# Key and value placement by DMA in the fourth layer of an attention kernel on one Trainium2 core

## What is computed

```python
residual = x
qt = conv1x1(x, w_q, b_q).reshape(BS * N_HEADS, H * W, -1)
xp = avg_pool_3x3_s2_same(x)                      # 8x8 tokens per image
kt = conv1x1(xp, w_k, b_k).reshape(BS * N_HEADS, H * W // 4, -1)
vt = conv1x1(xp, w_v, b_v).reshape(BS * N_HEADS, H * W // 4, -1)
attn = jnp.einsum('bnd,bmd->bnm', qt, kt) / TEMP  # d = 16
attn = jax.nn.softmax(attn, axis=-1)
out = jnp.einsum('bnm,bmd->bnd', attn, vt).reshape(BS, H, W, -1)
return conv1x1(out, w_o, b_o) + residual
```

## Time and profile before

| | |
|---|---|
| median of 3 runs | 147.38 us (146.55 to 152.97) |
| the profiled execution's own time | 146.52 us |
| its span in the trace | 144.6 us |
| PE busy | 132.7 us, 92% of the span |
| DVE busy | 105.5 us, 73% |
| ACT busy | 103.4 us, 72% |
| POOL busy | 57.4 us, 40% |

### The profile page before, as it was taken

One profiled execution on the slowest core, in us unless ns is written; L12 is line 12 of the kernel. 1 busy time (PEld: TensorE's weight loads), 2 busy tenths in 40 slices (PEclk: granted clock), 3 DMA queues, 4 the chain that ended last, 5 costly groups with the idle time before them and its releaser, 6 DMA issues.

```text
span 144.6 us, 4108 instructions
## 1 busy us (share of the span) xinstructions
PE 132.7 (92%) x1615; PEld 104.5 (72%) x1615; DVE 105.5 (73%) x249; ACT 103.4 (72%) x286; POOL 57.4 (40%) x91
## 2 busy tenths in 40 slices
PE   7677999999999999779698999999998999999991
PEld 4447999977676767555576996858665766899890
DVE  5775888998226979997588657799999997920062
ACT  0435734799883779869985599999899987676530
POOL 8941994000000000000078888105058776499000
PEclk9999999999999999999999999999999999999999
DMA  4950000000000000000000000000000000000036
GB/s 128 328 204 0 0 7 0 0 2 0 0 5 0 5 0 5 0 0 0 0 5 0 7 0 5 0 0 5 0 0 5 0 5 0 5 5 5 5 99 192
DMA packets 5026, 3.69 MB, mean 26 GB/s; under 512 B 400, under 2 KB 4880, under 8 KB 5008
## 3 DMA queue, kind: packets, MB, share of 16 engines
q1 hardware_dynamic: 3376, 1.78, 4.3%
q10 hardware_dynamic: 1632, 1.66, 3.6%
HBM read 2.39 MB, written 1.05 MB: 24 GB/s over the span
## 4 chain that ended last, share of the span: by engine, by line
PE 63%; DVE 26%; DMA 3%; issue 3%; POOL 1%; ACT 1%; ACTq 0%; DVEq 0%
PE bank L678 10%; PE bank L737 8%; PE bank L623 6%; PE bank L717 5%; PE bank L725 5%; DVE negmax L471 4%; PE bank L689 4%; DMA x_all<-in_x_dram 3%; DVE prob L480 3%; PE bank L662 3%; DVE prob L513 3%; PE bank L696 3%; PE bank L754 3%; DVE probT L494 3%; PE bank L609 2%
## 5 line engine op out<-in xcount | busy, mean ns | idle before, releaser
L332 ACT ACTIVATE prob<-bank,negmax 128x256 f32<-128x256 f32 (+1 forms) x48 | 19.4, 414 | 13.1 <-DVE negmax L471 12.8
L273 POOL TENSOR_TENSOR prob<-prob,inv 128x512 f32<-128x512 f32 x16 | 16.3, 1043 | 19.2 <-DVE inv L523 19.2
L285 POOL TENSOR_TENSOR prob<-xT 128x128 f32<-128x128 f32 x8 | 3.4, 419 | 49.5 <-DVE xT L504 49.4
L678 PE MATMUL bank<-probT,v 128*128 128x256 f32 x64 | 17.0, 388 | 1.8 <-issue 1.8
L623 PE MATMUL bank<-packed,xT 128*128 128x128 f32 x96 | 15.6, 287 | 1.0 <-ACT prob L332 1.0
L340 ACT ACTIVATE kdiag<-prob 32x512 f32<-32x512 f32 x24 | 15.0, 627 | 1.5 <-DVE prob L562 1.2
L717 PE MATMUL bank<-kdiag,qT 128*32 128x256 f32 x256 | 15.5, 382 | 0.0
L623 PEld LDWEIGHTS bank<-packed,xT 128*128 128x128 f32 x96 | 13.2, 191 | 2.9 <-issue 2.0
L678 PEld LDWEIGHTS bank<-probT,v 128*128 128x128 f32 x64 | 10.9, 190 | 4.6 <-issue 3.8
L501 DVE SCALAR_TENSOR_TENSOR xT<-bank,packed,xT 128x256 f32<-128x256 f32 x16 | 7.5, 482 | 7.8 <-PE bank L678 6.7
L471 DVE TENSOR_REDUCE negmax<-bank 128x2 f32<-128x512 f32 (+1 forms) x24 | 12.8, 534 | 0.5 <-PE bank L652 0.3
(11 more groups left out here) (92 smaller groups left out, 294.6 us busy)
## 6 DMA issues: line engine op xcount, KB each, us to landing
out_dram<-x_all SPq DMA_DIRECT2D x8, 128.0 KB, 1.9
packed<-in_pack_dram ACTq DMA_DIRECT2D x1, 708.5 KB, 6.9
x_all<-in_x_dram SPq DMA_DIRECT2D x2, 256.0 KB, 4.6
x_all<-in_x_dram ACTq DMA_DIRECT2D x2, 256.0 KB, 5.6
packed<-in_pack_dram SPq DMA_DIRECT2D x1, 198.0 KB, 5.9
packed<-in_pack_dram ACTq DMA_DIRECT2D x1, 192.0 KB, 6.2
packed<-in_pack_dram ACTq DMA_DIRECT2D x1, 160.0 KB, 3.2
packed<-in_pack_dram ACTq DMA_DIRECT2D x1, 48.0 KB, 5.8
```

The costliest lines, as they stand in the source:

```text
L273: nc.gpsimd.tensor_tensor(p, p, inv[g][:, t, :].unsqueeze(2).broadcast_to([128, HEADS, KEYS]), ALU.mult)\
L332: last = nc.scalar.activation(prob[g][:, t, 0:keys], psum("scores", layer, g)[:, keys * t:keys * t + keys], ACT.Exp, bias=negmax[g][:, t, ...
L678: last = mm(ps[:, 0:TOK], vals[:, k, :], probT[g][:, 0, TOK * k:TOK * k + TOK], start=k == 0, stop=k == TILES - 1)
```

## The change

The fourth layer's keys and values of a pair of images are each projected once, with unrepeated weights: one product of 128 columns for keys (channels on partitions) and one for values (tokens on partitions), in one bank. ACT adds the key bias into `kT`, DVE the value bias into `vt`. SP writes both to DRAM tensors `k_rows` and `v_rows`. It waits for each and places the keys with eight DMAs (one for each chunk's 16 partitions) into `kdiag`, now a block diagonal of all eight chunks, and the values with two DMAs into `vdiag`. Queries are unpadded: one product of 256 columns and one ACT instruction. A score product has 512 columns and there are 4 for a token tile instead of 8; its moving operand reads `kdiag` with a step of 128 elements (512 bytes) from one element to the next. There are two `kdiag` buffers instead of four, so pairs 2 and 3 wait for the scores of pairs 0 and 1 before they are placed. The step `vd` is gone. In the table `q` comes before `kv`, and `scores3` keeps its distance from `pool`.

```diff
-        steps += [("pool", 3, 1), ("kv", 3, 3), ("q", 3, 3), ("vd", 3, 1), ("scores3", 3, 1), ("share3", 3, 2), ("probT3", 3, 2),
+        steps += [("pool", 3, 1), ("q", 3, 3), ("kv", 3, 0), ("scores3", 3, 5), ("share3", 3, 2), ("probT3", 3, 2),
...
+            for step, layer, g in sequence:
+                if step == "kv":
+                    i = g // PAIR
+
+                    sp.wait_ge(s_key_rows, i + 1)
+                    sp.dma_start(k_dram[i], kT[i][:, :]).then_inc(s_keys_out[i], 16)
+                    wait_drained(sp, "kv", 3, g)
+                    sp.dma_start(v_dram[i], vt[i][:, :]).then_inc(s_vals_out[i], 16)
+                    if i == 0:
+                        sp.wait_ge(s_zero, QUARTERS + IMAGES // PAIR)
+                    if i >= KEY_BUFFERS:
+                        for t in range(TILES):
+                            wait_filled(sp, f"scores{t}", 3, PAIR * (i - KEY_BUFFERS) + PAIR - 1)
+                    sp.wait_ge(s_keys_out[i], 16)
+                    rows = k_dram[i].rearrange("(c e) n -> e c n", e=DH)
+                    for c in range(HEADS):
+                        sp.dma_start(kdiag[i % KEY_BUFFERS][DH * c:DH * c + DH, c, :, :], rows).then_inc(s_keys[i], 16)
+                    sp.wait_ge(s_vals_out[i], 16)
+                    rows = v_dram[i].rearrange("(j m) (c e) -> (m c) j e", m=HEADS, e=DH)
+                    for c2 in range(2):
+                        sp.dma_start(vdiag[i][KEYS * c2:KEYS * c2 + KEYS, :, c2, :], rows).then_inc(s_vals[i], 16)
...
-            def kv_strips(g):
-                for k in range(2):
-                    wait_drained(act, f"kv{k}", 3, g)
-                    for b in range(DVE_STRIPS, STRIPS):
-                        last = nc.scalar.activation(*kv_strip(g, k, b), ACT.Copy)
-                last.then_inc(s_strips_act, 1)
+            def keys3(g):
+                wait_filled(act, "kv", 3, g)
+                nc.scalar.activation(kT[g // PAIR][:, :], psum("kv", 3, g)[:, 0:PAIR * PTOK], ACT.Identity, bias=part["bk3"])\
+                    .then_inc(s_key_rows, 1)
...
+                mm(ps[:, 0:PAIR * PTOK], part["w3k"], pooled, start=True, stop=True)
+                mm(ps[:, PAIR * PTOK:PAIR * PTOK + C], pooled, part["w3v"], start=True, stop=True).then_inc(*filled_by("kv", 3, g))
```

More of the change, by code:

```diff
@@ L25 @@
 BIG = float(2 ** 100)
+KEY_BUFFERS = 2
 def constants():
@@ L142, in build @@
             for g in range(IMAGES):
-                if kind not in ("kv", "vd") and (kind, layer) not in (("qk", 1), ("qk", 2)):
+                if kind != "kv" and (kind, layer) not in (("qk", 1), ("qk", 2)):
                     due.append((start + g, -n, kind, layer, g))
@@ L248, in _ @@
             pool.wait_ge(s_half, 1)
-            for g in range(EARLY, IMAGES - LATE):
-                clear_kdiag(nc.gpsimd, g)
+            for n in range(EARLY, QUARTERS - LATE):
+                clear_kdiag(nc.gpsimd, n)
             for n in range(2):
@@ L262, in _ @@
                 nc.gpsimd.memset(windows[g], 0.0).then_inc(s_windows, 1)
-            for late in range(IMAGES - LATE, IMAGES):
+            for late in range(QUARTERS - LATE, QUARTERS):
                 clear_kdiag(nc.gpsimd, late)
@@ L525, in _ @@
             nc.vector.memset(warm_up[:, :], 0.0).then_inc(s_warm, 1)
-            for g in range(EARLY):
-                clear_kdiag(nc.vector, g)
+            for n in range(EARLY):
+                clear_kdiag(nc.vector, n)
             for g in range(HALF):
@@ L555, in _ @@
                         dve.wait_ge(s_packed[W3], 16)
[L556 to L568, removed]
+                    wait_filled(dve, "kv", 3, g)
+                    dve.wait_ge(s_key_rows, g // PAIR + 1)
+                    nc.vector.tensor_tensor(vt[g // PAIR][:, :], psum("kv", 3, g)[:, PAIR * PTOK:PAIR * PTOK + C], part["bv3"], ALU.add)\
+                        .then_inc(*drained_by("kv", 3, g))
                 if step == "scores3":
@@ L683, in keys_values3 @@
                 pe.wait_ge(s_pool, (g + 2) * POOL_STEPS)
[L684 to L687, removed]
-                        at = 128 * (c % half)
-                        last = mm(ps[:, at:at + 2 * PTOK], part["w3kv"][:, 128 * c:128 * c + 128],
-                                  poolT[g // 2][:, :, :, :].rearrange("p i h w -> p (i h w)"), start=True, stop=True)
-                    last.then_inc(*filled_by(f"kv{k}", 3, g))
@@ L693, in queries3 @@
[L693 to L706 removed]
+                ps, pooled = begin("kv", 3, g), poolT[g // PAIR][:, :, :, :].rearrange("p i h w -> p (i h w)")
@@ L711, in score3 @@
-                pe.wait_ge(s_strips_act, g // 2 + 1)
+                i = g // PAIR
+                pe.wait_ge(s_keys[i], 16 * HEADS)
                 ps = begin(f"scores{t}", 3, g)
-                for a in range(HALVES):
-                    for s in range(STRIPS):
-                        j = STRIPS * t + s
-                        key = KEYS * (HEADS * (g % 2) + j)
-                        last = mm(view(ps[STRIP * s:STRIP * s + STRIP, TOK * a:TOK * a + TOK], STRIPS),
-                                  qT[g][:, a, HTOK * j:HTOK * j + HTOK], kdiag[g // 2][:, :, key:key + KEYS], start=True, stop=True)
+                for s in range(STRIPS):
+                    j = STRIPS * t + s
+                    key = PTOK * (g % PAIR) + HKEY * j
+                    last = mm(ps[STRIP * s:STRIP * s + STRIP, :].rearrange("p (c m k) -> p c m k", c=HEADS, m=HKEY),
+                              qT[g][:, 0, HTOK * j:HTOK * j + HTOK],
+                              kdiag[i % KEY_BUFFERS][:, :, :, key:key + HKEY].rearrange("p c k m -> p c m k"), start=True, stop=True)
@@ L822, in _ @@
                     queries3(g)
-                if step == "vd":
-                    turn_values3(g)
                 if step == "scores3":
```

92 lines of the change are left out of this document (31 added, 61 removed).

## The result

The changed kernel takes 150.91 us (median of 4 runs, 149.86 to 151.86) against 147.08 us before (median of 4, 146.55 to 152.97). The ratio is 1.027 with a 95% interval from 1.018 to 1.037: slower, where 142.9 us and "faster" were the likeliest forecast; whether by 2% or more stays open, since the interval takes in 2%. The time lies in the stated range of 140.0 to 152.5 us. The profiled execution took 151.86 us with a span of 150.0.

A forecast was written before the change was run, and what follows sets the result against it. PE was taken to bound the kernel, DVE just under it. Of 12.3 us off PE, waits for keys take the rest: image 6 starting at 113.4 instead of 116.1, less 0.9, gives 146.5 - 3.6 = 142.9 us; range 140.0 to 152.5.

The forecast's parts named there:

- the fourth term of "What goes": Scores on PE: 16 records of 512 columns take 1.8 us an image instead of 1.86, 0.5 us saved for eight images.
- this rival: Scores' operand read at a 512-byte step halves its rate: 3.6 us an image, about 149 us in all; chance 0.18.
- the limit of 149.4: Upper limit of no change: a run tells about 2%, 2.9 us, from none, with limits 143.6 and 149.4 us.
- The work that goes: Savings on PE (12.3 us in all), on ACT (strip, value and query copies) and on DVE (5.4 + 3.5 us).
- The first pair's chain: First `kv` ends at 80.45, key store and placing DMAs follow, PE waits 2.2 us, first scores start at 88.2.
- The cycle: SP's work for each later pair, value issues, key store landing and eight placing issues: 8.4 us, longer than PE's 5 us.
- the straight line's 6: Value DMAs: extrapolating packet times by size gives 6 ns for a 64-byte packet; 20 ns was taken.
- Rival 1: Value packets hold the DMA rings: no gain at 30 ns a packet, 152.5 us at 45 ns; chance 0.17.
- The waits before images 0, 2 and 4: PE waits for keys before these images' scores: 2.2 us before image 0, about 3 us before images 2 and 4.
- the likeliest case: Cycle of 7 to 8.9 us and no stride penalty: 142.9 us, own range 141.5 to 144.5; chance 0.40.
- a sign of being wrong: Listed under what would show the forecast wrong: the granted clock below full in the fourth layer.
- PE's 12.3 us can't all be had: DVE's end can move by at most 5 us, so not all of PE's 12.3 us saving shortens the time.

The follow-up runs named there:

- e1: The changed kernel with the scores' operand read in runs of 8 elements, score columns in another order: 143.83 us, ratio to the kernel before 0.976.
- e5: The changed kernel with the operand read in runs of 8 elements and the product written into PSUM at a step of 8 elements: 143.65 us, ratio 0.967.
- e2: The kernel before, with the scores' moving operand read at a step of 2 elements (8 bytes) in each run of 64: 147.28 us.
- e4: The kernel before, with the scores' moving operand read at a step of 8 elements (32 bytes) in each run of 64: 167.90 us.
- e6: e1 without the two value DMAs into `vdiag` and PE's wait for them: 142.42 us, ratio 0.959.
- e9: e5 with a pair's value DMAs issued later, behind the next pair's key store: 142.92 us, ratio 0.967.
- e11: e9 with idle products on PE, 22 before image 0's scores and 12 before image 4's: 142.99 us, ratio 0.963.
- e7: e1 with four of a pair's eight key placing DMAs issued by ACT instead of SP: 149.39 us, ratio 1.009.
- e10: The changed kernel, stepped read kept, with a pair's value DMAs issued behind the next pair's key store: 150.52 us, ratio 1.021.

## Why the prediction was wrong

**The step that failed** is the fourth term of "What goes": "16 records of 512 columns ... so 16 take 1.8 us". It took the rate of contiguous runs for an operand with a step of 512 bytes. Measured: 3.55 us an image, 8 x 1.7 = 14 us more on PE. e1 and e5 show that this made the kernel slower than before: with runs of 8 the time is 143.8 and 143.7 us. Of the 14 us only 7 come back, because PE then waits for keys instead. The mechanism stood among the rivals, with the right size (3.6 us an image), but with a chance of 0.18. Its time was added up wrongly there: 146.5 - 12.3 + 14.4 + 2.2, the first wait, is 150.8 us and not about 149. The measured 150.9 is that sum, and it lies clear of the limit of 149.4 up to which half of this rival was counted as no change. My argument against it was that a float32 record takes two cycles a column, so a read may have room. e2 to e4 show where that room ends: a step of 2 elements fits in, a step of 4 doubles the time. The Trainium skill, "SBUF — State Buffer", section "Door 1: The DMA port swizzle", with its lines of 16 bytes, spoke for the rival, no row of the trace spoke against it, and I should have given it more than half.

**What held.** Point by point:
- The work that goes. ACT -20 us; DVE -6.5 us, where some 8 had been counted; on PE `q` -3.9 us and `vd` gone. The first pair's `kv` takes 0.45 us to the next operation, as forecast.
- The first pair's chain. From the end of the first `kv` to the first scores 7.7 us were forecast; in the changed kernel it is 8.0 (82.06 to 90.05), with PE's wait at 2.6 instead of 2.2 us. Key issues took 0.46 us each and value issues 0.66, near the 0.5 taken; placing DMAs landed after 2.5 us instead of the 1.8 taken.
- The cycle. Forecast 8.4 us, measured 7.7. The value packets took 10.6 ns and not 20, between the straight line's 6 and the 26 of the nearest row, so a small packet isn't dearer than a large one. By the forecast's own terms 9.4 ns less a packet should have shortened the cycle by 1.2 us; it fell by 0.7. The keys' issue began 3.9 us into the cycle (88.11 to 92.03) where that price gives 3.1, and why the key store was not back sooner isn't shown. Rival 1 is refuted: a packet is far from 30 ns. The Trainium skill, "DMA: Bandwidth & Descriptors", section "Specifications", has the DMA engine read, modify and write below 512 bytes; in these runs that didn't make a packet of 64 bytes dearer than one of 512, and whether it is part of the 10.6 ns can't be told.
- The waits before images 0, 2 and 4. Absent in the changed kernel but for the first, since stepped scores gave the DMAs time; there in e1 at 2.8, 2.3 and 2.7 us, where 2.2 and about 3 had been forecast.
- The forecast's total. e1 and e5 are the kernel that the likeliest case described, and take 143.8 and 143.7 us against 142.9. That they come so near is partly luck. In e1's profile the first `kv` is 0.9 us later than forecast and one stretch of 3.4 us at half clock costs about 1.5 us; from image 0 to image 6 it still takes 24.9 us against 25.2, as the cycles were forecast too long. I had given a falling clock a price nowhere, named it with waits over 4 us in rival 1 and listed it as a sign of being wrong; it came behind waits of 2.6 to 3 us, in the changed kernel too.
- "PE's 12.3 us can't all be had" stands: e6, without the value DMAs, gets 5 to 6 us of them and e5 4 to 5.

What stays open: how much of the remaining waits could be had. e9 and e11 removed one wait each in their profiles and the ratios didn't move beyond their intervals. What makes the stepped read slow isn't shown, only from which step on. All scores here are products on four column strips at once; whether a product alone in the array would pay as well wasn't tried.

## What to carry to other kernels

Before counting an operand's columns, look at the step between neighbouring elements that PE reads: from 16 bytes on, this float32 product, on four column strips at once, took twice the time. If the order has to change somewhere, change it where the product is written into PSUM, which cost nothing in e5, and not in PE's read or DVE's write. And when a rule speaks against a change and no row of the trace shows the case, the absence of a row is no argument for the change.

## What the runs showed of the hardware that was not expected

- For float32 products on four strips the price of a stepped read sets in between 8 and 16 bytes: the scores' group took 15.5 us contiguous, 16.2 at 8 bytes, 30.6 at 16 and 31.1 at 32.
- Half clock didn't slow the stepped scores: 3.54 us at a granted clock of 0.51 and 3.55 at full, where contiguous ones went from 1.85 to 3.34 us.
- A stepped write into PSUM of 32 bytes cost PE nothing (1.85 us), while DVE writing with the same step went from 692 to 1110 ns.
- A 64-byte DMA packet cost 10.6 ns, one of mostly 512 bytes 25 ns. In e7, with two queues issuing keys and values at once, the 16 engines were full for 22% more bytes a second than in e1, and key DMAs landed after up to 4.6 us.
- Waits of PE of 2.3 to 3 us were followed in several runs by some 3 us at half the granted clock (the changed kernel 91.0, e1 105.9, e5 97.7, e11 97.0), and in others not (e1 89.6 and 97.4, e5 89.4, e10 89.2).
